# The attention step's turns moved from TensorE to DMA, its order rewritten, and a router of 16 matmuls

## The chip, the cores and the metric

One core of a Trainium2 chip runs the whole kernel. Its engines are TensorE (PE, with its weight loads shown as PEld), VectorE (DVE), ScalarE (ACT), GpSimd (POOL), and SyncE (SP), which here only issues DMAs. The metric is the device time of one execution in microseconds (us), and of several executions the median is given.

## The reference

The input x is 2 x 2048 tokens of 512 channels. It is a block with attention and a mixture of experts side by side, cut here to what matters:

```
xn  = layernorm(x)
# attention: 16 heads of 32, chunks of 128 tokens, decay rate s per head
h   = rmsnorm(xn) * qkv_norm_w ;  qkv = h @ ternary(qkv_w).T
per chunk:  scores = (q k^T) * mask            # decay within a chunk
            o      = scale * (scores v + (q * lam_t) S)
            S      = lam_T * S + (k * lam_rev)^T v
out = rmsnorm(rmsnorm(o) * norm_w) * proj_norm_w @ ternary(proj_w).T
# experts: 8, the best 2 per token; and one shared network of width 1024
probs    = softmax(xn @ w_gate) ; best two, weights renormalised
routed   = sum over the two of  w * ((silu(g) * u) @ w_down),  g, u = xn @ w_gate_up
shared   = (silu(xn @ g_sh) * (xn @ u_sh)) @ w_sh_down
result   = x + out + routed + shared
```

## The kernel before, in words

Matmuls take 16-bit floats for speed; for accuracy each activation is split in a high part and a low rest (both f16). Attention projections multiply both parts with the exact ternary weight. The router and the experts also split their weights and use three of the four products (`PASSES`).

The program has five stages. **Setup** (to about 50 us) makes the ternary weights, the masks and the scaled router weights. **Attention** (50 to about 548 us) runs 16 steps; a step handles chunk n of both batch rows (u = 0, 1), that is 256 tokens, and beside it prepares chunk n+1 (its projections) and n+2 (its layer norm). **Shared, first half** sends eight steps of tokens through the shared network and computes the routing. **Routed** takes 72 tiles of 128 rows, gathered by expert. **Shared, second half** does the other tokens and adds up.

Each engine has an order written out by hand in a function `step(q, par, ...)` (n = 2q + par), and waits are semaphores. An engine never overtakes a waiting instruction of its own list. PE fills three PSUM banks in turn, the ring: the class `Ring` lists the fills of a step in `STEP`, position i takes bank i mod 3, and `fill` makes PE wait until the content three positions earlier has been read. The names are xnT (turned input), kTr (turned keys), ot (outputs), kv (outer products), q, k, v (projections), rt (router), onT (turned normalised output) and proj. Scores have four banks of their own (`sc`), in two pairs; before, a set is four matmuls that fill the first half of a pair's banks, and four sets (`scores(u, ..., sets)`) make one u. `decayed_scores` (VectorE, line 1026) multiplies a set with the mask and writes probs.

Turns. PE turns xn (`xn_turn`, line 624), ScalarE copies xnT, makes hh (line 822) and the high half of x16 (line 814), VectorE makes hl (line 972), GpSimd the low half of x16 (line 1160). The normalised output is turned by `o_turn` (line 727), and `y_high`, `y_low` split it. `masked_kv` (VectorE, line 1043) multiplies the outer products with a block mask. SP's list of a step: load xl of n+2, load xr, store xn, four slices of the expert weights (`load_weights`, whose largest magnitude VectorE takes in `weight_maxima`), store x1 for u = 0, store xT, store x1 for u = 1. In the routed stage GpSimd gathers a tile's 128 rows of xn (f32) by an index copied by VectorE; ScalarE and GpSimd split them in halves (lines 1918, 1850), and SP turns them by DMA (`dma_start_transpose`, line 1823).

## Time and profile before

| what | value |
|---|---|
| median of 3 runs | 1400.04 us (1399.59 to 1403.44) |
| the profiled execution | 1401.92 us, its span 1400.2 us |
| granted clock of TensorE, mean | 0.973 of full speed |
| busy: PE, DVE, ACT, POOL | 91%, 50%, 37%, 38% of the span |
| DMA | 195.06 MB, mean 139 GB/s |

The profile is one execution; a busy time is the time in which an engine worked on an instruction. A group of instructions is named by the line of the kernel that issued it, its engine, and output <- inputs. Matmuls overlap, and the duration shown of one (0.38 us for 512 columns) is longer than the distance from its start to the next one's start; the distance is what it costs.

### The profile page before, as it was taken

The numbers are of one execution on the slowest core, as the hardware profiler recorded it, in microseconds if no ns is written. First come the engines' busy times: TensorE is split into PE (matmuls) and PEld (weight loads), VectorE is DVE, ScalarE is ACT, GpSimd is POOL, SyncE is SP. The second block draws the span as 40 slices with busy tenths as digits, with TensorE's granted clock in tenths as the row PEclk, the third lists the DMA queues.
The fourth block names the chain that finished last, engine by engine and source line by source line (L and its number), as shares of the span: only waits on it lengthen the run. The fifth ranks groups of instructions, "written<-read, shape, count | busy, mean of one in ns | idle before, by whom it ended". The sixth has DMA issues, their size and how long they took to land. (4 is left out here: it accounts for less than half of the span.)

```text
span 1400.2 us, 29499 instructions
## 1 busy us (share of the span) xinstructions
PE 1281.1 (91%) x10418; PEld 879.9 (63%) x10418; DVE 695.2 (50%) x1606; ACT 514.0 (37%) x1034; POOL 527.0 (38%) x467
## 2 busy tenths in 40 slices
PE   1499999999999994999999969999999969999997
PEld 1477777667776673777777734444444447777775
DVE  4477877878878766883333322222222213333323
ACT  3444444444444434432323224544445411111111
POOL 0333344333444332024541035555554542444333
PEclk9699999999999997999999989999999989999999
DMA  5213443334433334524552358888888861443333
GB/s 173 95 60 129 154 145 109 109 131 142 161 109 109 131 125 162 180 93 105 107 138 102 33 136 183 188 194 190 186 191 186 192 190 65 179 164 135 135 136 121
DMA packets 174072, 195.06 MB, mean 139 GB/s; under 512 B 100976, under 2 KB 107248, under 8 KB 174000
## 3 DMA queue, kind: packets, MB, share of 16 engines
q1 hardware_dynamic: 158464, 156.17, 38.0%
q0 software_dynamic: 13328, 37.04, 10.0%
q8 instruction: 55, 0.90, 0.3%
q10 hardware_dynamic: 2208, 0.82, 0.2%
q14 instruction: 17, 0.14, 0.0%
HBM read 117.55 MB, written 56.77 MB: 124 GB/s over the span
## 5 line engine op out<-in xcount | busy, mean ns | idle before, releaser
L1269 PE MATMUL gu<-xT,WG 128*128 128x256 f16 x3072 | 350.3, 275 | 23.5 <-DMA x1s<-x_dram 11.8
L1269 PEld LDWEIGHTS gu<-xT,WG 128*128 128x128 f16 x3072 | 302.7, 99 | 74.8 <-DVE WD L1556 12.4
L1280 PE MATMUL rgu<-WG,raw 128*128 x876 | 215.1, 382 | 14.4 <-issue 10.9
L1695 DVE SCALAR_TENSOR_TENSOR actv<-gu,up_inv,sg 128x512 f32<-128x512 f32 x64 | 48.0, 751 | 252.8 <-ACT sg L1532 252.6
L1532 ACT ACTIVATE sg<-gu,gate_inv 128x512 f32<-128x512 f32 x64 | 43.9, 686 | 319.2 <-PE gu L1269 319.2
L1287 PE MATMUL yp<-WD,ah 128*128 128x512 f16 x512 | 152.3, 379 | 1.0 <-DVE al L1700 1.0
L1280 PEld LDWEIGHTS rgu<-WG,raw 128*128 128x128 f16 x876 | 86.1, 98 | 105.5 <-issue 23.2
L1850 POOL TENSOR_TENSOR xsp<-xg,xsp 128x512 f16<-128x512 f32 x75 | 86.7, 1157 | 105.2 <-ACT xsp L1918 105.2
L655 PE MATMUL ring<-hh,qkvT 128*128 128x256 f16 x512 | 116.4, 276 | 6.0 <-DVE hl L972 6.0
L1250 POOL DMA_INDIRECT xg<-xn_dram,idx x77 | 73.8, 958 | 123.9 <-POOL xsp L1850 66.4
L655 PE MATMUL ring<-hl,qkvT 128*128 128x256 f16 x512 | 116.4, 275 | 0.0
L1765 POOL DMA_INDIRECT raw<-y_dram,gidx x64 | 63.6, 994 | 133.7 <-DVE ys L1676 105.4
L1970 DVE TENSOR_TENSOR alr<-rat,ahr 128x256 f16<-128x256 f32 x72 | 30.5, 424 | 160.0 <-ACT ahr L1938 160.0
L1160 POOL TENSOR_TENSOR x<-xnT,x 128x1024 f16<-128x1024 f32 x16 | 34.3, 2142 | 198.8 <-ACT x L814 198.8
L1749 POOL DMA_INDIRECT slot_dram<-payload,posi x64 | 62.8, 981 | 116.5 <-DVE posi L1645 57.8
L1287 PE MATMUL yp<-WD,al 128*128 128x512 f16 x256 | 97.0, 379 | 0.0
L1026 DVE SCALAR_TENSOR_TENSOR probs<-sc,r,mask 128x512 f32<-128x512 f32 x128 | 89.7, 742 | 3.4 <-PE sc L671 3.4
L1287 PE MATMUL ryp<-WD,ahr 128*128 x288 | 85.9, 379 | 0.0
L1287 PEld LDWEIGHTS yp<-WD,ah 128*128 128x128 f16 x512 | 49.7, 98 | 49.3 <-DVE al L1700 2.5
L1924 ACT ACTIVATE raw<-ryp,out_inv 128x512 f32<-128x512 f32 x72 | 49.5, 687 | 65.9 <-PE ryp L1287 65.9
L1183 POOL TENSOR_TENSOR on<-on,pnw_b 128x512 f32<-128x512 f32 x32 | 40.7, 1273 | 77.1 <-DVE on L1065 77.1
L1700 DVE TENSOR_TENSOR al<-actv,ah 128x512 f16<-128x512 f32 x64 | 46.5, 726 | 44.5 <-ACT ah L1535 44.5
(237 smaller groups left out, 2163.2 us busy)
## 6 DMA issues: line engine op xcount, KB each, us to landing
y_dram<-raw SPq DMA_DIRECT2D x72, 256.0 KB
xl<-in_L_attn_x SPq DMA_DIRECT2D x16, 512.0 KB, 4.5
xn_dram<-xn SPq DMA_DIRECT2D x16, 512.0 KB, 6.4
wraw<-in_L_ffn_w_gate_up SPq DMA_DIRECT2D x16, 512.0 KB, 6.9
xT_dram<-x SPq DMA_DIRECT2D x16, 512.0 KB, 2.8
xr<-in_L_attn_x SPq DMA_DIRECT2D x16, 512.0 KB, 5.9
x_dram<-x SPq DMA_DIRECT2D x32, 256.0 KB, 2.1
xT<-xT_dram SPq DMA_DIRECT2D x16, 512.0 KB, 6.9
```

The lines of the kernel that those rows point to most:

```text
L655: ins = pe.matmul(bank[:, g * T2:(g + 1) * T2], qkvT[:, kk, a:a + P], h[:, kk, :], start=(kk == 0 and h is hh), stop=(kk == KT - 1 and h i ...
L1026: v.scalar_tensor_tensor(out=probs[:, u, s].rearrange("p (j g) t -> p j (g t)", j=2), in0=sc[:, 2 * pair:2 * pair + 2, 0:2 * P], scalar=r[ ...
L1250: pool.indirect_dma_start(out=xg[:, par], out_offset=None, in_=xn_dram, in_offset=bass.IndirectOffsetOnAxis(ap=idx[:, par, 0:1], axis=0)). ...
L1269: ins = pe.matmul(gu[:, h, f * tokens:(f + 1) * tokens], w[:, kk, b, a0:a0 + P], x[:, kk, a], start=(kk == 0 and (a, b) == PASSES[0]), sto ...
L1280: ins = pe.matmul(gu[bank][:], x(kk, a), w[:, 0, kk, b, :], start=(i == 0), stop=(i == len(done) - 1))
L1287: ins = pe.matmul(y[:], act_hl[a][:, f, :], w[:, f, b, :] if len(w.shape) == 4 else w[:, 0, f, b, :], start=(first and f == 0 and (a, b) = ...
L1695: v.scalar_tensor_tensor(out=actv[:, g % 2], in0=gu[g % 2][:, 1].rearrange("p (f t) -> p f t", f=FT), scalar=up_inv[:, 1:2], in1=sg[:], op ...
L1700: v.tensor_tensor(al[:, g % 2], actv[:, g % 2], ah[:, g % 2], ALU.subtract).then_inc(S["al_ready"], 1)
L1749: pool.indirect_dma_start(out=slot_dram, out_offset=bass.IndirectOffsetOnAxis(ap=posi[:, kk, t:t + 1], axis=0), in_=payload[:, kk, t, :], ...
L1765: pool.indirect_dma_start(out=gy[:, u, i], out_offset=None, in_=y_dram, in_offset=bass.IndirectOffsetOnAxis(ap=gidx[:, u, i:i + 1], axis=0 ...
L1850: pool.tensor_tensor(xsp[:, par, 1], xg[:, par], xsp[:, par, 0], ALU.subtract).then_inc(S["low_ready"], 1)
L1924: act.activation(ysb[:, par], yp[par][:], ACT.Copy, scale=out_inv[:, 0:1]).then_inc(S["y_ready"], 1)
```

## The change

All turns in attention are made by DMA. ScalarE, VectorE and GpSimd first write the high and low f16 halves in the untransposed layout side by side (xs for the router and the experts, hs for the projections, ys for proj), and SP issues six DMA transposes of 128 x 1024 f16 in a step: `turn_h` twice, `turn_x` twice, `turn_y` twice. The norm weight of h is now multiplied on GpSimd (`weighted_h`) into hn. The ring loses xnT and onT and gets a new order of 15 names, and the steps of all engines are reordered. A score call is now one pair of whole banks, 8 matmuls, and `decayed_scores` does 1024 elements at once, twice per u. ScalarE copies the diagonal blocks of the outer products (`take_kv`, four copies per u, into kvm cleared once) in place of the masked multiplication on VectorE. The state's decay becomes an operation of its own (`decay`).

The router's matmuls take both halves of its weights side by side as one operand of 16 columns for the high part of x (4 per u) and the high half alone for the low part (4 per u): 16 matmuls for 24. VectorE adds the two sums (`take_logits`), and the scale `ginv` moves into the exponential of the softmax.

The token rows stored for the gather are now the two f16 halves (xs_dram, as many bytes as before). The routed stage gathers them four tiles ahead and turns them directly: the index copies, ScalarE's `high_part` and GpSimd's `low_part` go. In x16, xT_dram and the shared stages the two batch rows u lie apart, so the moving operand of the q, k and shared matmuls is two pieces of 128 columns.

The fragments below come in this order: the ring; SP's new functions and its step; PE's router, scores and step; VectorE's logits, scores and step; GpSimd's weighted_h and step; the routed stage's gather and turn.

```diff
--- before
+++ after
...
     BANKS = 3
-    FRONT = ["xnT0", "xnT1", "q0", "q1", "rt", "k0", "k1", "v0", "v1"]
-    STEP = ["xnT0", "xnT1", "kTr0", "ot0", "kv0", "q0", "q1", "kTr1", "ot1", "rt", "onT0", "k0", "kv1", "k1", "proj0",
-            "onT1", "v0", "v1", None, None, "proj1"]
-    LAST = ["kTr0", "ot0", "kv0", "kTr1", "ot1", "onT0", "kv1", "proj0", "onT1", "proj1"]
+    FRONT = ["q0", "q1", "rt", "k0", "k1", "v0", "v1", None, None]
+    STEP = ["kTr0", "ot0", "kTr1", "kv0", "ot1", "q0", "q1", "k0", "rt", "k1", "v0", "proj0", "kv1", "v1", "proj1"]
+    LAST = ["kTr0", "ot0", "kTr1", "kv0", "ot1", "proj0", "kv1", "proj1"]
...
+            def turn_h(q, par):
+                n = 2 * q + par
+                if not (isinstance(n, int) and n == 0):
+                    wait_apart(sp, S["v_ready"], 2 * n, S["sp_passed"])
+                for u in range(B):
+                    wait_apart(sp, S["hl_ready"], 2 * n + u + 1, S["sp_passed"])
+                    sp.dma_start_transpose(hT[:, u], hs[:, u].rearrange("p a c -> p (a c)")).then_inc(hT_in[u], 16)
+            def turn_x(q, par):
+                n = 2 * q + par
+                if not (isinstance(n, int) and n < 2):
+                    wait_apart(sp, S["logits_ready"], n - 1, S["sp_passed"])
+                    wait_apart(sp, xT_out[par], 16 * q, S["sp_passed"])
+                for u in range(B):
+                    wait_apart(sp, S["xlow_ready"], 2 * n + u + 1, S["sp_passed"])
+                    sp.dma_start_transpose(x16[:, par, u], xs[:, u].rearrange("p a c -> p (a c)")).then_inc(xT_in[u], 16)
...
+            def turn_y(u, q, par):
+                n = 2 * q + par
+                wait_apart(sp, S["yl_ready"], 2 * n + u + 1, S["sp_passed"])
+                sp.dma_start_transpose(yT[:, u], ys[:, u].rearrange("p a c -> p (a c)")).then_inc(yT_in[u], 16)
...
                 if norm:
                     sp.wait_ge(S["xn_ready"], 2 * n + 2)
                     load_xl(q + 1, par)
-                if not front:
+                if front:
+                    turn_h(*after(q, par))
+                    turn_x(*after(q, par))
+                    store_xs(*after(q, par))
+                    sp.wait_ge(S["wmax_ready"], n)
+                    load_weights(*after(q, par))
+                else:
                     for g in range(2):
                         load_group(sp, k, g)
                 sp.wait_ge(S["x1_ready"], 2 * n)
                 load_xr(q, par)
+                for u in range(B):
+                    turn_y(u, q, par)
+                store_x1(0, q, par)
                 if front:
-                    store_xn(*after(q, par))
-                    sp.wait_ge(S["wmax_ready"], n)
-                    load_weights(*after(q, par))
-                for u in range(B):
-                    if u == 1 and front:
-                        store_xT(*after(q, par))
-                    sp.wait_ge(S["x1_ready"], 2 * n + u + 1)
-                    dst = x1_steps[n] if isinstance(n, int) else x1_steps[bass.ds(n, 1)][0]
-                    sp.dma_start(dst[:, u], x1[:, u]).then_inc(x1_out[u], 16)
+                    store_xT(*after(q, par))
+                store_x1(1, q, par)
...
             def router(q, par, st):
                 n = 2 * q + par
-                pe.wait_ge(S["xlow_ready"], n + 1)
+                for u in range(B):
+                    pe.wait_ge(xT_in[u], 16 * (n + 1))
                 bank, done = fill(pe, "rt", st)
                 for u in range(B):
+                    both = slice(2 * u * EXPERTS, 2 * (u + 1) * EXPERTS)
                     for kk in range(KT):
-                        for i, (a, b) in enumerate(PASSES):
-                            ins = pe.matmul(bank[:, u * EXPERTS:(u + 1) * EXPERTS], x16[:, par, kk, a, u * P:(u + 1) * P],
-                                            wg16[:, kk, b, :], start=(kk == 0 and i == 0), stop=(kk == KT - 1 and i == 2))
+                        pe.matmul(bank[:, both], x16[:, par, u, kk, :], wg16[:, kk].rearrange("p b e -> p (b e)"),
+                                  start=(kk == 0), stop=False, skip_group_check=True)
+                    for kk in range(KT):
+                        ins = pe.matmul(bank[:, 2 * u * EXPERTS:(2 * u + 1) * EXPERTS], x16[:, par, u, KT + kk, :],
+                                        wg16[:, kk, 0, :], start=False, stop=(kk == KT - 1), skip_group_check=True)
                 ins.then_inc(done, 1)
...
-            def scores(u, q, par, sets):
-                n = 2 * q + par
-                if u == 0 and sets[0] == 0:
+            def scores(u, q, par, pair):
+                n = 2 * q + par
+                if u == 0 and pair == 0:
                     pe.wait_ge(S["q_ready"], 2 * n + 2)
                     pe.wait_ge(S["k_ready"], 2 * n + 2)
-                for s in sets:
-                    pair = s % 2
-                    pe.wait_ge(sc_free[pair], 4 * n + 2 * u + s // 2)
-                    for gg in range(2):
-                        for jj in range(2):
-                            g, j = 2 * (s // 2) + gg, 2 * pair + jj
-                            rows = slice(HD * j, HD * j + HD)
-                            ins = pe.matmul(sc[:, j, gg * P:(gg + 1) * P], kT[rows, par, g, u * P:(u + 1) * P],
-                                            qT[rows, par, g, u * P:(u + 1) * P], start=True, stop=True)
-                    ins.then_inc(sc_full[pair], 1)
+                pe.wait_ge(sc_free[pair], 2 * n + u)
+                for g in range(KT):
+                    for j in (2 * pair, 2 * pair + 1):
+                        rows = slice(HD * j, HD * j + HD)
+                        ins = pe.matmul(sc[:, j, g * P:(g + 1) * P], kT[rows, par, g, u * P:(u + 1) * P],
+                                        qT[rows, par, g, u * P:(u + 1) * P], start=True, stop=True)
+                ins.then_inc(sc_full[pair], 1)
...
                 nxt = after(q, par)
-                if front:
-                    xn_turn(0, *nxt, st)
-                    xn_turn(1, *nxt, st)
                 k_turn(0, q, par, st)
-                scores(1, q, par, (0, 1))
+                scores(1, q, par, 0)
                 outputs(0, q, par, st)
-                scores(1, q, par, (2, 3))
+                scores(1, q, par, 1)
+                k_turn(1, q, par, st)
+                o_back(0, q, par)
                 outer(0, q, par, st)
-                o_back(0, q, par)
+                outputs(1, q, par, st)
                 if front:
                     project("q0", *nxt, st)
+                o_back(1, q, par)
+                if front:
                     project("q1", *nxt, st)
-                k_turn(1, q, par, st)
-                outputs(1, q, par, st)
+                    project("k0", *nxt, st)
+                    router(*nxt, st)
+                    project("k1", *nxt, st)
+                    project("v0", *nxt, st)
+                    scores(0, *nxt, 0)
+                proj(0, q, par, st)
                 if front:
-                    router(*nxt, st)
-                o_back(1, q, par)
-                o_turn(0, q, par, st)
-                if front:
-                    project("k0", *nxt, st)
+                    scores(0, *nxt, 1)
                 outer(1, q, par, st)
                 if front:
-                    project("k1", *nxt, st)
-                proj(0, q, par, st)
-                if front:
-                    scores(0, *nxt, (0, 1))
-                o_turn(1, q, par, st)
-                if front:
-                    project("v0", *nxt, st)
-                    scores(0, *nxt, (2, 3))
                     project("v1", *nxt, st)
                 proj(1, q, par, st)
...
                 bank = filled(v, "rt", st)
                 dst = logits[:, :, n, :] if isinstance(n, int) else logits[:, :, bass.ds(n, 1), :][:, :, 0, :]
-                v.tensor_scalar(dst, bank[:, 0:B * EXPERTS].rearrange("p (u e) -> p u e", u=B), ginv[:, 0:1], None, ALU.mult
-                                ).then_inc(S["logits_ready"], 1)
+                parts = bank[:, 0:2 * B * EXPERTS].rearrange("p (u b e) -> p u e b", u=B, b=2)
+                v.tensor_reduce(dst, parts, AX.X, ALU.add).then_inc(S["logits_ready"], 1)
...
-                    v.wait_ge(sc_full[pair], 4 * n + 2 * u + s // 2 + 1)
-                    v.scalar_tensor_tensor(out=probs[:, u, s].rearrange("p (j g) t -> p j (g t)", j=2),
-                                           in0=sc[:, 2 * pair:2 * pair + 2, 0:2 * P],
+                for pair in range(2):
+                    v.wait_ge(sc_full[pair], 2 * n + u + 1)
+                    v.scalar_tensor_tensor(out=probs[:, u, pair].rearrange("p j g t -> p j (g t)"),
+                                           in0=sc[:, 2 * pair:2 * pair + 2],
                                            scalar=r[:, par, u:u + 1],
-                                           in1=mask[:, 4 * s:4 * s + 4].rearrange("p (j g) t -> p j (g t)", j=2),
+                                           in1=mask[:, 8 * pair:8 * pair + 8].rearrange("p (j g) t -> p j (g t)", j=2),
                                            op0=ALU.mult, op1=ALU.mult).then_inc(sc_free[pair], 1)
...
                 scaled_k(0, q, par, st)
-                decayed_scores(1, q, par, (0, 1))
-                if front:
-                    h_low(*nxt)
-                decayed_scores(1, q, par, (2, 3))
-                weight_maxima(q, par, (1, 2, 3))
-                masked_kv(0, q, par, st)
+                decayed_scores(1, q, par)
                 o_mean(0, q, par)
+                scaled_k(1, q, par, st)
                 normed(0, q, par)
                 if has_norm:
                     row_stats(0, q + 1, par)
                     row_stats(1, q + 1, par)
-                scaled_k(1, q, par, st)
-                second_norm(0, q, par)
+                weight_maxima(q, par, (1, 2, 3))
+                o_mean(1, q, par)
+                if has_norm:
+                    norm_stats(q + 1, par)
+                normed(1, q, par)
+                y_low(0, q, par)
+                weight_maxima(q, par, (0,))
+                for u in range(B):
+                    second_norm(u, q, par)
+                for u in range(B):
+                    second_factor(u, q, par)
                 if front:
                     take_logits(*nxt, st)
-                y_low(0, q, par, st)
-                o_mean(1, q, par)
-                normed(1, q, par)
+                y_low(1, q, par)
                 if has_norm:
-                    norm_stats(q + 1, par)
-                masked_kv(1, q, par, st)
-                second_norm(1, q, par)
-                weight_maxima(q, par, (0,))
+                    norm_factors(q + 1, par)
+                    norm(q + 1, par)
+                residual(0, q, par, st)
                 if front:
-                    decayed_scores(0, *nxt, (0, 1))
-                residual(0, q, par, st)
-                if has_norm:
-                    norm(q + 1, par)
-                y_low(1, q, par, st)
-                if front:
-                    decayed_scores(0, *nxt, (2, 3))
+                    decayed_scores(0, *nxt)
                 else:
                     weight_scales()
+                if has_norm:
+                    h_low(q + 1, par)
                 residual(1, q, par, st)
-                if has_norm:
-                    norm_factors(q + 1, par)
...
+            def weighted_h(q, par):
+                n = 2 * q + par
+                for u in range(B):
+                    pool.wait_ge(S["xn_ready"], 2 * n + u + 1)
+                    if not (isinstance(n, int) and n == 0):
+                        pool.wait_ge(S["hl_ready"], 2 * n + u - 1)
+                    pool.tensor_tensor(hn[:, u], xn[:, par, u], hw_b[:], ALU.mult).then_inc(S["hn_ready"], 1)
...
                     x_low(*after(q, par))
+                decay(0, q, par)
                 weighted(0, q, par)
+                decay(1, q, par)
+                weighted(1, q, par)
                 update(0, q, par)
+                if norm:
+                    weighted_h(q + 1, par)
                 if front:
                     decayed_q(*after(q, par))
-                weighted(1, q, par)
                 update(1, q, par)
...
+        def gather(pool, r):
+            pool.indirect_dma_start(out=xg[:, r % XG], out_offset=None, in_=xs_dram,
+                                    in_offset=bass.IndirectOffsetOnAxis(ap=slots[:, r, 0:1], axis=0)
+                                    ).then_inc(xg_in[r % XG], 16)
...
                                     in_=payload[:, kk, t, :], in_offset=None).then_inc(slot_out, 16)
-                        for par in range(2):
-                            gather(pool, 0, par, S["pool_passed"])
+                        pool.wait_ge(split, PIECES * (GROUPS + EXPERTS - 1))
+                        pool.wait_ge(slot_in, 16)
+                        for r in range(XG):
+                            gather(pool, r)
...
-                        wait_apart(sp, S["low_ready"], r + 1, S["sp_passed"])
-                        sp.dma_start_transpose(xh[:, i % XH], xsp[:, i % 2].rearrange("p a c -> p (a c)")
-                                               ).then_inc(turned[i % 2], 16)
...
```

## Rows read from the trace of the kernel before

**Rows 1.** The page: busy us of each engine, share, instructions.
```profile
PE 1281.1 (91%) x10418; PEld 879.9 (63%) x10418; DVE 695.2 (50%) x1606; ACT 514.0 (37%) x1034; POOL 527.0 (38%) x467
```

**Rows 2.** Windows: length, busy us (instructions) of each engine, clock, DMA share, GB/s.
```profile
822.00:1112.00 290.00, 286.36 (x1374) 137.66 (x1375) 74.56 (x274) 140.47 (x273) 144.92 (x137) 0.99 0.83 185
...
79.48:519.93 440.45, 423.84 (x4674) 320.12 (x4674) 347.88 (x836) 197.62 (x463) 173.45 (x120) 1.00 0.36 125
```

**Rows 3.** Order of time, PE, one attention step: start, us, then the instruction.
```profile
343.32 1.04 PE L624 MATMUL ring<-ident,xn 128*128 128x128 f32 x8
344.33 0.66 PE L679 MATMUL ring<-ident,kT 128*128 128x128 f32 x4
344.91 0.74 PE L671 MATMUL sc<-qT,kT 32*128 32x128 f32 x16
345.58 1.16 PE L689 MATMUL ring<-qlam,state 128*128 128x128 f32 x8
...
349.79 0.27 PE L655 MATMUL ring<-hh,qkvT 128*128 128x256 f16 x1
...
353.28 0.60 PE L679 MATMUL ring<-ident,kT 128*128 128x128 f32 x4
...
355.71 0.76 PE L634 MATMUL ring<-wg,x 128*128 128x8 f16 x24
356.50 0.66 PE L709 MATMUL o_ps<-ident,oT 128*128 128x128 f32 x4
356.99 0.60 PE L727 MATMUL ring<-ident,on 128*128 128x128 f32 x4
357.43 0.27 PE L655 MATMUL ring<-hh,qkvT 128*128 128x256 f16 x1
...
364.31 0.66 PE L727 MATMUL ring<-ident,on 128*128 128x128 f32 x4
364.80 0.38 PE L648 MATMUL ring<-qkvT,hh 128*128 128x512 f16 x1
...
366.88 1.37 PE L671 MATMUL sc<-qT,kT 32*128 32x128 f32 x16 [0.19 <-DVE probs L1026]
...
368.29 0.38 PE L648 MATMUL ring<-qkvT,hh 128*128 128x512 f16 x1
...
369.79 0.38 PE L648 MATMUL ring<-qkvT,hl 128*128 128x512 f16 x1
...
371.04 0.38 PE L736 MATMUL ring<-projT,yh 128*128 128x512 f16 x1 [0.87 <-ACT vS L832]
```

**Rows 4.** Groups by line: xcount | busy us, mean ns, then idle before.
```profile
L1026 DVE SCALAR_TENSOR_TENSOR probs<-sc,r,mask 128x512 f32<-128x512 f32 x128 | 89.7, 742 | 3.4 <-PE sc L671 3.4
...
L1183 POOL TENSOR_TENSOR on<-on,pnw_b 128x512 f32<-128x512 f32 x32 | 40.7, 1273 | 77.1 <-DVE on L1065 77.1
...
L988 DVE TENSOR_REDUCE wmax<-wraw 128x1024 f32 x12 | 14.5, 1206 | 0.0
```

**Rows 5.** DMA: transposes on SP; queue in 900 to 950, then 330 to 390.
```profile
L1823 SPq DMA_TRANSPOSE raw<-xsp x75: 1232/1246/2240, 816.6 to 1128.0; - x75
...
DMA to landing us min/median/max: 3.0/3.1/5.2
...
q1 hardware_dynamic: 14358, 6.28, 58.8%
...
q1 hardware_dynamic: 3648, 7.60, 36.9%
```

**Rows 6.** Start of the routed stage, PE and SP; PE's waits in it.
```profile
822.16 6.48 PE L1280 MATMUL rgu<-WG,raw 128*128 x18 [10.89 <-issue]
...
816.58 15.87 SPq L1823 DMA_TRANSPOSE raw<-xsp  x4
...
PE rgu L1280 <- DMA raw<-xsp: 3.4, 7, 0.8
```

**Rows 7.** Order of time, PE, first projection of the attention block.
```profile
61.49 0.39 PE L655 MATMUL ring<-hh,qkvT 128*128 128x256 f16 x1 [5.99 <-DVE hl L972]
```

414 lines of the change are left out of this document (184 added, 230 removed).

## Prediction

> **What bounds the kernel now.** I read the page's busy times first [rows 1]: TensorE (PE) works 91% of the span, no other engine more than half. An average hides stages, so next the windows by stage [rows 2]: from the first attention step's k_turn to the last one's, PE is busy 423.84 of 440.45 us at the full 2.4 GHz (granted clock 1.00), and in the routed stage 286.36 of 290.00 (0.99). Both stages are PE's. DMA's share is 0.36 in the first and 0.83 in the second. Hence a removed PE instruction is worth its issue time, and work put on other engines is free until it makes PE wait. Third, the order of time inside one attention step [rows 3]. The window of rows 2 holds 15 steps, so one takes 29.36 us. It shows what PE does, start to start, and the only two stalls: before the fourth score set and before proj1. I say once: about 0.3% (4 us) is what a measurement here can tell from none.
>
> **Part 1, PE work of one step, all from [rows 3].** xn_turn goes: 343.32 to 344.33, 1.01 us. The two o_turns go: 356.99 to 357.43 and 364.31 to 364.80, 0.93 us. The router: 24 matmuls from 355.71 to 356.50 are 0.033 us each; 16 leave 0.53, so 0.26 us less. The bound from below is the same 0.79 (no gain, if 16 columns cost double); it is a quarter microsecond either way. Scores: a free set of 8 matmuls takes 344.91 to 345.58, 0.67 us; the one in front of v1 takes 366.88 to 368.29, 1.41, waiting in its middle for VectorE's probs. The new pairs use whole banks with two row groups alternating, as inside a set now, so I take 0.67: 0.74 less. v0 starts at 364.80, is 8 matmuls at 0.215 (368.29 to 369.79 is seven), and so ends 366.52; scores start at 366.88. Of this gap 0.2 goes. proj1 waits for ScalarE to empty v1's bank: v1 ends at 370.01, proj1 starts at 371.04, 1.03 us. In the new ring proj1 is index 14 and takes the bank of proj0 (11), which residual(0) read long before. It goes whole. The sum is 4.17 us. From 29.4 that leaves PE 25.3 us.
>
> **Part 2, the other engines in those 25.3 us.** VectorE's h_low becomes two full-width operations, at most 0.74 each like a probs operation [rows 4]; masked_kv leaves it; eight probs operations of 742 ns become four of twice the width (bounds 0.74 and 1.48; a weight maximum over 1024 elements takes 1206 ns [rows 4], and I take 1.28 as the nearest). It was busy about 23 us a step and comes to about 21. GpSimd gains weighted_h, 2 of on's shape at 1273 ns, 2.5 us on some 11.7: 14.2. ScalarE takes take_kv (eight small copies, at most 0.4 each) for the two xnT and some scaled copies: even. None is a bound. I also followed the lists by hand: VectorE makes ys(0) ready about 15 us into a step, ScalarE has every bank empty when PE asks (k1 and v0 with under 1 us to spare), GpSimd's qlam is ready about 1 us before outputs(0). These are estimates with little slack.
>
> **Part 3, the DMA turns; here lies the uncertainty.** A step gains six transposes of 256 KB on SP's queue. In the routed stage, in 50 us, the hardware queue was busy 58.8% (29.4 us) with 12 transposes and 13 stores [rows 5]. Plain transfers move 7.60 MB in 36.9% of 60 us, 343 GB/s, so a 256 KB store is 0.76 us, 13 are 9.9, and a transpose is (29.4-9.9)/12 = 1.63 us of all 16 engines. Issue to landing is 3.1 us, 1.25 of it SP's [rows 5]. So the six cost 9.8 us beside plain traffic of 11.1 (22.1 over two steps): 20.9 us in 25.3, a share of 0.83. The routed stage carries just that share and PE loses little [rows 2, 6]. SP itself issues six at 1.25 and ten plain at about 0.5: 12 us, room enough.
> The row and a rule differ here. The Trainium skill (Advanced Engine Details and Errata, X-Bar Transpose (TRN2)) says transposes are as fast as regular DMAs; by that each is 0.76 us, the queue never makes PE wait, and the result would be rival B's. The trace disagrees, with 1.63 beside 0.76, but in a stage where gathers share the engines.
> What matters is order. SP's list is strict, and one queue serves in turn. SP enters step n only when residual(1) of n-1 is done, about 1.2 us after PE started n (VectorE still has h_low for u = 1 ahead of it, which waits for ScalarE to take v1). I put the first bytes at about 2.7, an estimate: the issue and half of what lies between a transpose's issue end and its landing. Service by then: x1 0.76, xl 1.5, two hT, two xT, xs 1.5, the four weight slices (1.18 MB) 3.4, xr 1.5, then yT(0). PE asks for hT (q0) at 7.9: today k_turn(0) to q0 is 344.33 to 349.79, 5.46, and k_turn(1) with outputs(1), which now stand ahead of q0 too, is 353.28 to 355.71, 2.43 [rows 3]. hT lands at 2.7+2.26+2x1.63 = 8.2: 0.3 late. PE asks for yT(0) at 18.4 (q0 with q1 is 349.79 to 353.28, 3.49; k0 with k1 the same; o_back 0.5, router 0.53, v0 1.72, scores 0.67). It lands at 2.7+8.66+5x1.63 = 19.5: 1.1 late, the first included. yT(1) has 4 us slack. So the step becomes 25.3+1.1 = 26.4 in strict order and 25.3 if the order is softer; I take 26.2. In general it is 25.3 + max(0, 5s-7.0) for a transpose of s us.
> Gain: 15 x (29.36-26.2) = 47.4 us.
>
> **Part 4, the ends.** Start: today q0 begins 61.49, after a wait of 5.99 for hl [rows 7]. New: xn 53.0, hn by GpSimd 1.27 twice, hs high and low, two transposes with nothing ahead of them (wraw is behind turn_x): about 60.4. Step 0 then has its weight loads late. I put 0, bounds -1.5 to +3. Last step: yT(0) sits behind 3 MB of group weights, and proj(0) then runs cold; but residual(1) waits for the weight scales chain anyway. +1, bounds 0 to +4. Routed start: PE begins at 822.16 after 10.89 idle; the first transpose is issued at 816.58 [rows 6], behind ACT's and GpSimd's split of the gathered rows; now it can go as soon as SP has issued the block's two loads: -1.1, bounds -0.3 to -2.5. Routed steady state: GpSimd's and ScalarE's splitting of each tile's rows leaves; neither sets PE's pace, only the 3.4 us that PE waited for a transpose, 7 times [rows 6]: -1, bounds +1 (transposes unchanged) to -3.4. Everything else I cost at nothing: ginv moves into the exponential's scale, bmask and qnw_c are setup work behind weight loads, ten index copies are gone from VectorE. The two-piece moving operand (2 x 128) in the q, k and 3072 shared matmuls I also put at 0: each piece is still unit stride. Its upper bound, taken as slow as one of xn_turn's 128-column transposes (8 in 1.01, 0.126 each) instead of the 0.109 of q's 32 in 3.49 [rows 3], is +52 us for the shared part.
>
> **Sum.** 47.4 - 0 - 1 + 1.1 + 1 = 48.5 us less. Against the profiled execution's own 1401.92 (span 1400.2): 1353.4. The median of the runs is 1400.04, 1.9 below it: 1351.5, say 1352.
>
> **Rivals.** A, the forecast: transposes just late, step 25.8 to 26.9; 1342 to 1362; 0.46.
> B: transposes cost nearly what plain transfers cost or overlap them, step 25.3 (5s-7.0 negative): 15 x 4.06 = 60.9 gained, 1338. For it: the 3.1 us landing is flat even at share 0.83. 0.22.
> C: the queue or a chain with little slack (qlam, k1's bank) costs 2 to 3.5 us a step, step 27.3 to 28.8: 1368 to 1391, centre 1378. For it: landing reached 5.2 us at most [rows 5], and bursts cluster at each step's start. 0.20.
> D, slower than before: the transposes throttle the queue. Every step's hT and yT hang on SP's strict list, which waits for the last residual, so lateness is paid in each step and not made up. It passes today's 29.36 once 5s-7.0 exceeds 4.1, s = 2.2 us. At s = 2.6 the step is 31.3 and the time 1429. Against it: the measured 1.63 includes contention. 0.08.
> E: the two-piece operand costs half its bound in the shared stages, +25: 1377. Nothing in the trace speaks for it. 0.04.
> Likeliest is A: 1352. The range 1336 to 1378 takes B, A and the better half of C. Slower by over 0.3%: most of D, 0.07; within: 0.03; faster: 0.90.
>
> **What the changed profile would show.** Step period (k_turn to k_turn) about 26.2, PE idle in it 1 us, released by the DMAs of hT and yT and not by ACT vS; no stall at proj1; scores 0.67 both times; router 0.53. DMA share in attention 0.75 to 0.85. Routed tiles at the same pace, PE starting about 1 us sooner after its gap. Shared matmuls still spaced 0.109. I am wrong if PE waits there for probs, kS or the state, or if hT lands after 9 us into the step.

## The result, and the profile after

The median is 1360.03 us (4 runs, 1358.43 to 1364.50) against 1400.37 us for the kernel before in the same session (4 runs, 1399.59 to 1403.44). The ratio is 0.9713, with a 95% interval of 0.9686 to 0.9741: faster, by 40 us. The forecast was 1352, with a range of 1336 to 1378 and 0.90 on faster. The profiled execution took 1360.6 us, its span 1358.8, at a mean granted clock of 0.975.

The page's busy times, to be read beside [rows 1]:

```profile
PE 1252.2 (92%) x10034; PEld 865.4 (64%) x10034; DVE 648.2 (48%) x1396; ACT 479.2 (35%) x1039; POOL 488.3 (36%) x437
```

Windows of the same two stages as [rows 2], each from its first to its last matmul or k_turn:

```profile
790.47:1095.80 305.33, 302.75 (x1452) 146.26 (x1452) 74.12 (x216) 110.59 (x215) 64.33 (x68) 0.99 0.79 181
...
78.03:482.91 404.88, 401.61 (x4321) 309.27 (x4321) 306.57 (x716) 201.28 (x538) 218.76 (x163) 1.00 0.74 197
```

The 15 steps take 404.88 us, 26.99 each, where they took 440.45, 29.36 each. PE is busy in all but 3.3 us of them, so the step is almost pure PE work, and DMA's share has doubled to 0.74. PE's waits from 80 to 490 us are these two alone:

```profile
PE ring L751 <- DMA yT<-ys: 2.8, 4, 1.2
PE ring L682 <- issue: 0.5, 1, 0.5
```

Order of time on PE, beside [rows 3]; the first four lines are of the step whose k_turn is at 322.21, the others of the next one, whose k_turn is at 348.95:

```profile
322.21 0.60 PE L704 MATMUL ring<-ident,kT 128*128 128x128 f32 x4
322.74 1.16 PE L696 MATMUL sc<-qT,kT 32*128 32x128 f32 x16
323.83 1.16 PE L714 MATMUL ring<-qlam,state 128*128 128x128 f32 x8
...
330.84 1.37 PE L682 MATMUL ring<-hT,qkvT 128*128 128x256 f16 x11
...
363.27 0.25 PE L657 MATMUL ring<-wg,x 128*128 128x16 f16 x4
363.38 0.24 PE L660 MATMUL ring<-wg,x 128*128 128x8 f16 x4
...
363.68 1.91 PE L682 MATMUL ring<-hT,qkvT 128*128 128x256 f16 x16
...
368.33 1.90 PE L751 MATMUL ring<-projT,yT 128*128 128x512 f16 x8
```

Three things stand here. A score set takes 322.74 to 323.83, 1.09 us, where a free set took 0.67 [rows 3]. The router takes 363.27 to 363.68, 0.41 (forecast 0.53). And q0 starts 8.63 us into the step. SP's queue in the same step tells how near the edge that is:

```profile
323.49 0.33 SPq L589 DMA_DIRECT2D x_dram<-x  x1
324.03 0.41 SPq L552 DMA_DIRECT2D xl<-in_L_attn_x  x1
324.76 2.96 SPq L567 DMA_TRANSPOSE hT<-hs  x2
...
337.03 4.22 SPq L606 DMA_TRANSPOSE yT<-ys  x2
```

The second transpose of hs is issued at 326.2, and the longest of the two landings is 4.2 us: hT is there at 330.4, 0.4 us ahead of q0. That is 8.2 us into the step, as forecast. In the 9 us around yT the 16 DMA engines are taken nearly all the time (window 334 to 343, DMA share 0.97; the share is a sum of packet times and reads up to 1.25 in a stretch of another run below, so 1 is not a hard ceiling):

```profile
334.00:343.00 9.00, 9.00 (x88) 6.56 (x87) 7.33 (x30) 4.99 (x15) 4.18 (x3) 1.00 0.97 238
```

The span's 41.4 us are divided so, read from PE's first instructions of each stage:

| stage | change, us | forecast |
|---|---|---|
| up to the first k_turn (79.48, now 78.03) | -1.5 | 0 |
| 15 steps | -35.6 | -47.4 |
| last step, k_turn to the first shared matmul (35.65, now 40.35) | +4.7 | +1 |
| shared stages, both halves | -0.7 | 0 |
| gap ahead of the routed stage (10.89, now 11.68) | +0.8 | -1.1 |
| routed tiles | -0.7 | -1 |
| gap behind the routed stage (11.71, now 3.24) | -8.5 | 0 |

The last step, on PE:

```profile
499.90 3.31 PE L751 MATMUL ring<-projT,yT 128*128 128x512 f16 x8 [6.92 <-DMA yT<-ys]
503.05 1.05 PE L742 MATMUL ring<-vS,kS 128*128 128x128 f32 x8
503.94 1.89 PE L751 MATMUL ring<-projT,yT 128*128 128x512 f16 x8
523.26 1.01 PE L1294 MATMUL gu<-xT,WG 128*128 128x256 f16 x4 [17.43 <-DMA x1s<-x_dram]
```

GpSimd and VectorE in the same stretch:

```profile
505.39 1.26 POOL L1203 TENSOR_TENSOR state<-state,kvm 128x512 f32<-128x512 f32 x1 [6.44 <-ACT kvm L855]
512.89 0.39 POOL L1233 PARTITION_ALL_REDUCE wall<-wtop  x1 [6.24 <-issue]
```

```profile
503.92 0.21 DVE L1022 TENSOR_REDUCE wtop<-wmax 128x4 f32<-128x64 f32 x1
513.32 0.17 DVE L1024 TENSOR_SCALAR wall<-wall 128x4 f32<-128x4 f32 x1 [9.19 <-POOL wall L1233]
```

VectorE has the maxima ready at 504.1, but GpSimd still has its last state update, which hangs on outer(1), behind the late proj(0). The all-reduce shows 6.24 us after that update, and residual(1), the store and the reload of x1 stand behind it. In the kernel before, the update was done at 539.4, ahead of wtop, and VectorE waited 5.06 us:

```profile
538.11 1.27 POOL L1178 TENSOR_TENSOR state<-state,kvm 128x512 f32<-128x512 f32 x1
545.20 0.39 POOL L1201 PARTITION_ALL_REDUCE wall<-wtop  x1 [5.82 <-issue]
```

```profile
540.36 0.20 DVE L1004 TENSOR_REDUCE wtop<-wmax 128x4 f32<-128x64 f32 x1
```

The gap behind the routed stage, PE, after:

```profile
1099.20 2.08 PE L1294 MATMUL gu<-xT,WG 128*128 128x256 f16 x13 [3.24 <-PEq L1803]
```

### The profile page after: what moved, and what is told of

Its sections match the earlier page's. It is cut to its first block and busy times, and to the rows that moved or that the text cites. A ratio compares the mean times of both kernels' runs of the same rounds, so it can differ in the third digit from the quotient of the medians.

```text
span 1358.8 us, 27803 instructions
## 1 busy us (share of the span) xinstructions
PE 1252.2 (92%) x10034; PEld 865.4 (64%) x10034; DVE 648.2 (48%) x1396; ACT 479.2 (35%) x1039; POOL 488.3 (36%) x437
## 5 line engine op out<-in xcount | busy, mean ns | idle before, releaser
L1275 POOL DMA_INDIRECT raw<-xs_dram,slots x73 | 69.2, 948 | 295.9 <-DMA raw<-raw 238.6
L682 PE MATMUL ring<-hT,qkvT 128*128 128x256 f16 x1024 | 121.6, 275 | 19.7 <-DMA hT<-hs 19.3
L682 PEld LDWEIGHTS ring<-hT,qkvT 128*128 128x128 f16 x1024 | 98.6, 99 | 34.8 <-issue 22.9
L1043 DVE SCALAR_TENSOR_TENSOR probs<-sc,r,mask 128x1024 f32<-128x1024 f32 x64 | 80.5, 1279 | 35.7 <-PE sc L696 35.3
L1208 POOL TENSOR_TENSOR on<-on,pnw_b 128x512 f32<-128x512 f32 x32 | 46.8, 1463 | 101.4 <-DVE on L1075 101.4
L696 PE MATMUL sc<-qT,kT 32*128 32x128 f32 x1024 | 73.6, 283 | 0.7 <-issue 0.7
L696 PEld LDWEIGHTS sc<-qT,kT 32*128 32x128 f32 x1024 | 61.7, 186 | 19.5 <-issue 19.5
L1946 DVE SCALAR_TENSOR_TENSOR actvr<-rgu,cw,sgr 128x256 f32<-128x256 f32 x72 | 34.8, 484 | 78.5 <-ACT sgr L1921 78.5
```

The lines of the kernel that those rows point to most:

```text
L682: ins = pe.matmul(bank[:, g * T2:(g + 1) * T2].rearrange("p (u t) -> p u t", u=B), qkvT[:, kk, w0:w0 + P], hT[:, :, a * KT + kk, :], start ...
L696: ins = pe.matmul(sc[:, j, g * P:(g + 1) * P], kT[rows, par, g, u * P:(u + 1) * P], qT[rows, par, g, u * P:(u + 1) * P], start=True, stop= ...
L1043: v.scalar_tensor_tensor(out=probs[:, u, pair].rearrange("p j g t -> p j (g t)"), in0=sc[:, 2 * pair:2 * pair + 2], scalar=r[:, par, u:u + 1],
L1208: pool.tensor_tensor(on3[:, u], on[:, u], pnw_b[:], ALU.mult).then_inc(S["on3_ready"], 1)
L1275: pool.indirect_dma_start(out=xg[:, r % XG], out_offset=None, in_=xs_dram, in_offset=bass.IndirectOffsetOnAxis(ap=slots[:, r, 0:1], axis=0 ...
```

## The experiments

All ratios are to the kernel before. In the listings by step, the period is the first k_turn to the sixteenth, over 15.

**Score sets.** A set in the kernel after runs 8 matmuls of 32 rows over two row groups (j) of the array; the sets before used all four in one call. Two kernels change the order alone. In the first, both pairs go as one run of 16 matmuls:

```diff
                 for g in range(KT):
-                    for j in (2 * pair, 2 * pair + 1):
+                    for j in range(HPT):
...
-                ins.then_inc(sc_full[pair], 1)
+                        if g == KT - 1 and j % 2 == 1:
+                            ins.then_inc(sc_full[j // 2], 1)
```

> The changed kernel with the two score pairs of one u issued as one run of 16 matmuls, g outside and all four row groups j = 0..3 inside; VectorE's operations stay. Theory R (the score sets grew from 0.67 to 1.09 us because a call now alternates between two row groups only, where it went over all four before): the 16 matmuls take about 1.1 us in place of 2 x 1.09, the step falls from 26.75 to 24.6 if no other wait appears, 1325 us in all; VectorE and the turn of y are then within 0.5 us of the path, so up to 1335. Rival W (the price comes from filling whole banks, or from 128 columns of 32 rows as such): 16 matmuls still take 2.2 us, step 26.7, 1360 us.

Measured: 1357.98 us, ratio 0.9689 (0.9664 to 0.9714). Its order of time on PE:

```profile
321.70 1.17 PE L697 MATMUL sc<-qT,kT 32*128 32x128 f32 x32
322.80 1.16 PE L716 MATMUL ring<-qlam,state 128*128 128x128 f32 x8
...
330.75 1.91 PE L682 MATMUL ring<-hT,qkvT 128*128 128x256 f16 x16 [1.61 <-issue]
```

Sixteen matmuls take 1.10 us, as long as eight did. So the mechanism holds, and 2.2 us of PE work a step are gone. But the time hardly moves (2 us, less than the intervals of the two kernels), and the period is 27.09 (76.56 to 482.98): the saved time is now a wait of q0, 24.8 us in 13 waits from 80 to 480 us. The view names no releaser for it (`issue`), but the weight load beside it waits for the DMA of hT. The second kernel lets neighbours share a row group:

```diff
-                for g in range(KT):
-                    for j in (2 * pair, 2 * pair + 1):
+                for j in (2 * pair, 2 * pair + 1):
+                    for g in range(KT):
```

> The changed kernel with the two loops of a score call exchanged: j outside, g inside, so that neighbours in the queue use the same row group. Theory R: two row groups overlapped before, now hardly any; a call takes 1.6 to 1.75 us in place of 1.09, step 26.75 + 4 x 0.6 = 29.1, about 1397 us. Rival W (nothing overlapped in the changed kernel anyway): unchanged, 1.09 us and 1360 us.

Measured, in a single run: 1390.72 us, period 28.94 (78.75 to 512.90), no PE wait. A set:

```profile
368.74 1.71 PE L696 MATMUL sc<-qT,kT 32*128 32x128 f32 x16
```

So 8 such matmuls cost 1.7, 1.09 or 0.55 us with one, two or four row groups in turn. The Trainium skill (TensorE: Matmul & The Clock Gate, Why this matters for your kernels) says small-K matmuls run concurrently when each lands in a distinct row group, with a factor of 3.07 for four; the trace agrees, with 1.71 over 0.55.

**The last step.** outer(1) and ScalarE's copies of kv(1) go ahead of proj(0) and of y_high(1), in the last step only:

```diff
-    LAST = ["kTr0", "ot0", "kTr1", "kv0", "ot1", "proj0", "kv1", "proj1"]
+    LAST = ["kTr0", "ot0", "kTr1", "kv0", "ot1", "kv1", "proj0", "proj1"]
...
+                if not front:
+                    outer(1, q, par, st)
                 proj(0, q, par, st)
...
+                if not front:
+                    take_kv(1, q, par, st)
                 y_high(1, q, par)
```

> The changed kernel with, in the last attention step only, outer(1) ahead of proj(0) on TensorE (kv1 before proj0 in the ring) and take_kv(1) ahead of y_high(1) on ScalarE. Theory L: the last step lost 4.7 us because GpSimd's all-reduce of the weight maxima comes 6.2 us after its last state update, which waited for outer(1), which waited behind proj(0) for the turned y. Then the all-reduce starts 4 to 6 us sooner and the time is 1355. Rival Y (the turned y itself ends the stage): proj(1) and residual(1) stay the end and the time stays 1360.

Measured: 1349.94 us, ratio 0.9640 (0.9622 to 0.9657). GpSimd's last update and all-reduce:

```profile
502.25 1.26 POOL L1207 TENSOR_TENSOR state<-state,kvm 128x512 f32<-128x512 f32 x1 [0.32 <-ACT kvm L857]
509.30 0.39 POOL L1237 PARTITION_ALL_REDUCE wall<-wtop  x1 [5.78 <-issue]
```

From k_turn to the first shared matmul it is now 33.6 us (485.89 to 519.49) in place of 40.35, although proj(0) starts no earlier. The order was the cause of the 4.7, and 2 us more were there to be had. The medians say 10 us, this stretch 6.7; the rest isn't placed. The profiled execution is the slowest of that kernel's five (1356.53 us), and its last k_turn came 3 us later than in the kernel after.

**SP's list.** What held hT in the first experiment? The row of SP there has hT issued at 325.60, 4.43 us after k_turn, behind the store of x1(1) (324.33) and the load of xl (324.86); in the kernel after it was 2.55. The store waits for residual(1), which ends VectorE's list behind probs and h_low. VectorE at the end of that step (the next k_turn is at 347.58):

```profile
343.60 0.75 DVE L1104 SCALAR_TENSOR_TENSOR x<-ring,g,xr 128x512 f32<-128x512 f32 x1 [1.71 <-PE ring L753]
344.27 2.47 DVE L1041 SCALAR_TENSOR_TENSOR probs<-sc,r,mask 128x1024 f32<-128x1024 f32 x2
346.65 3.26 DVE L990 TENSOR_TENSOR hs<-raw,hs 128x512 f16<-128x512 f32 x2
349.84 0.74 DVE L1104 SCALAR_TENSOR_TENSOR x<-ring,g,xr 128x512 f32<-128x512 f32 x1
```

VectorE waits for proj(0) on PE and then works through to residual(1) without a gap; v1 and ScalarE's part of hs don't hold it. Its two h_low operations take 3.26 us here and 1.92 in the kernel after: GpSimd works beside them nearly all the time here and under half of it there.

First both edits together, without touching SP:

> The kernel after with both earlier edits: score pairs as 16 matmuls over four row groups, and in the last step outer(1) and its copies ahead of proj(0) and y_high(1). Theory A (the two edits act in different places and add): the steps keep the period of the four-group kernel, 26.41 us with q0 waiting for hT, and the shared stage starts about 10 us earlier; 1360 - 2 - 10 = 1348 us. Theory B (the shorter last step of the second edit gave its gain only because that kernel's other steps ran late): 1355 us or more.

Measured: 1348.79 us, ratio 0.9647 (0.9629 to 0.9664), period 27.01. The score order is again worth 1 us, which is less than the intervals can tell, and the two edits together are worth what the shorter last step is worth alone. (The 26.41 in the expectation was one step, read off a timeline; the mean over 15 of that kernel is 27.09.) Now SP turns hs for the step after next as soon as it is there:

```diff
                 if front:
-                    turn_h(*after(q, par))
+                    if isinstance(q, int) and n == 0:
+                        turn_h(0, 1)
                     turn_x(*after(q, par))
...
                 if front:
                     store_xT(*after(q, par))
+                if norm:
+                    turn_h(q + 1, par)
                 store_x1(1, q, par)
```

> As the kernel with both edits, and SyncE issues the two transposes of hs for the step after next ahead of the store of x1(1) and of the load of xl, not behind them. In the four-group kernel x1(1) was ready at 323.43, its store went out at 324.33 and hT was issued at 325.60, while hs was whole about 322.8. Theory S (SyncE's list in strict order behind residual(1) makes hT late): hT is issued about 2 us earlier, the wait of q0 (1.6 to 2.5 us at 13 of 15 steps) is gone or under 0.5, the period falls from 26.41 to 25.1 to 25.8, and the time is 9 to 18 us below the kernel with both edits: 1330 to 1339. Theory T (the time that the transposes take under load, or VectorE and ScalarE that make hs, set hT): q0 still waits over 1 us, period over 26.1, 1344 to 1350.

Measured: 1324.99 us, ratio 0.9461 (0.9446 to 0.9477). SP in one step, whose k_turn is at 329.57:

```profile
329.63 2.93 SPq L567 DMA_TRANSPOSE hT<-hs  x2
332.85 0.34 SPq L589 DMA_DIRECT2D x_dram<-x  x1
333.89 0.40 SPq L552 DMA_DIRECT2D xl<-in_L_attn_x  x1
```

And the window of its 15 steps:

```profile
77.32:455.01 377.69, 370.83 (x4321) 281.16 (x4321) 314.45 (x716) 202.11 (x538) 228.54 (x163) 1.00 0.81 211
```

hT is issued 0.06 us into this step and within 1.3 us of k_turn in the others, q0 no longer waits, and the period is 25.18. The list was the wait. What PE still waits for in the 15 steps is mostly yT, 4.3 us in 7 waits. One could still think that ScalarE's order of making hs is next, so the high half of h(0) was put ahead of the copies of kv(1):

> As the last one, and ScalarE takes the high half of h(0) ahead of the copies of kv(1) (1.10 us). If VectorE and ScalarE that make hs are what holds hT after SyncE's order is mended, another 0.2 to 1 us per step goes, 3 to 15 us in all. If not, it is the same within 3 us, or up to 5 us slower, because kvm(1) and with it GpSimd's update of the state come 0.6 us later.

Measured: 1324.36 us, ratio 0.9460 (0.9437 to 0.9484), period 25.14: the same. And the fourth corner, SP's new order with the old score sets:

> The shorter last step and SyncE's transposes of hs ahead of the store of x1(1), but the score sets as in the kernel after (8 matmuls over two row groups each). It is the fourth corner of a square: scores in sets or pairs, SyncE's order old or new. Known corners, all with the shorter last step: sets and old order 1350, pairs and old order 1349, pairs and new order 1325. Theory S (in the kernel after PE's own 26.99 us per step hide a late hT; only when the scores are shorter does SyncE's order show): 1350 within 2 us, period 26.9 to 27.0, so neither edit is worth anything alone and both together 24 us. Rival (the order alone pays, because it also calms the transfers around yT or the other queues): 1335 to 1345.

Measured: 1351.45 us, ratio 0.9654 (0.9627 to 0.9680), period 26.78. With the shorter last step in all four, the square is:

| | SP's order of after | hs turned first |
|---|---|---|
| score sets, two row groups | 1349.94 | 1351.45 |
| score pairs, four row groups | 1348.79 | 1324.99 |

Neither edit alone is worth anything that the intervals can tell, both together 25 us. Two bounds of 27 us lay on top of each other: PE's own work, and the loop q0, proj(0), residual(0), probs and h_low, residual(1), SP's list, hT, q0. That the order of SP's list is the weak link of the loop is shown by the square; its other links are read from the rows above.

**What a transpose costs.** Two more per step, of a constant tile into a spare one, in the kernel after:

```diff
                     turn_x(*after(q, par))
+                    turn_spare(0, n)
                     store_xs(*after(q, par))
...
                 load_xr(q, par)
+                if front:
+                    turn_spare(1, n)
                 for u in range(B):
                     turn_y(u, q, par)
```

> The kernel after with two more transposes of the same shape per step (of a constant tile into a spare one that nobody reads), one behind those of x, one ahead of those of ys: eight in place of six. The prediction put one at 1.63 us of all 16 engines: 3.3 us per step more on 19.97 (0.74 of 26.99), so the DMA share rises from 0.74 to 0.84 to 0.86, yT lands 1.3 us or more later against a slack of some 1.1 us, proj(0) waits 0.3 to 1.5 us in most steps, and the time rises by 5 to 22 us to 1365 to 1382. Rival (transposes are cheap, half of that or less): share 0.77 to 0.80, no wait, 1360 within 3 us.

Measured: 1424.97 us, ratio 1.0174 (1.0158 to 1.0191): slower than the kernel before, and far above the 1365 to 1382 expected. Its windows over the 15 steps, over the wait for one late proj(0) and over that proj(0), then PE's order of time there:

```profile
77.00:548.30 471.30, 433.31 (x4321) 321.12 (x4322) 306.61 (x716) 201.16 (x538) 218.01 (x163) 0.92 0.74 186
...
352.60:354.70 2.10, 0.00 (x0) 0.00 (x1) 0.31 (x1) 0.00 (x0) 2.09 (x2) 1.00 1.25 261
354.70:358.30 3.60, 3.60 (x10) 1.13 (x11) 0.00 (x0) 0.00 (x0) 2.85 (x2) 0.53 0.12 23
```

```profile
349.60 1.89 PE L687 MATMUL ring<-qkvT,hT 128*128 128x512 f16 x8
...
354.70 3.56 PE L763 MATMUL ring<-projT,yT 128*128 128x512 f16 x8 [2.12 <-DMA yT<-ys]
```

The period is 31.42: 4.4 us more, of which the wait in front of proj(0) is 2.1 here, and 1.7 is that the eight matmuls behind it take 3.49 (354.70 to 358.19) and not 1.8. The granted clock of that stretch is 0.53, so the engine is at 1.2 of its two levels (1.2 and 2.4 GHz) for nearly all of it. By the windows of all 15 steps, PE idles 2.3 us a step more than in the kernel after and is busy 2.1 us more with the same matmuls. One part of the lateness isn't load: the second spare transpose stands ahead of ys in SP's own list too, and yT is issued at 348.91, 15.8 us after k_turn in place of 14.8. With one more transpose only, behind those of x:

> The kernel after with one more transpose per step, behind those of x; none directly ahead of those of ys. With two more (the second directly ahead of ys) each step was 4.4 us longer and the time 65 us. Theory O (what stands directly ahead of ys in the queue decides: its 16 engines are 0.97 busy from 334 to 343 us of the kernel after, and less before that): the extra work drains ahead of ys, proj(0) waits 0 to 0.3 us, and the time is 1360 to 1366. Theory L (the load of all transfers decides, each transpose alike): half of the 65 us or near it, proj(0) waits in most steps, 1385 to 1395. In both the DMA busy time per step rises by 1.6 to 1.8 us.

Measured: 1384.89 us, ratio 0.9888 (0.9869 to 0.9906). PE waits 17.6 us for yT in 14 waits from 80 to 480 us, and the window of its steps is:

```profile
77.95:506.30 428.35, 408.98 (x4321) 311.68 (x4322) 306.51 (x716) 201.16 (x538) 218.28 (x163) 0.98 0.76 195
```

DMA busy time per step is share times period. With the share of the queue to three digits over the same windows it is 0.740 x 26.99 = 19.97 us in the kernel after, 0.755 x 28.56 = 21.56 with one more and 0.735 x 31.42 = 23.09 with two. One transpose is 1.6 us of all 16 engines; the forecast had 1.63. That it costs twice a plain transfer isn't only contention: in the trace of the kernel after, over the 15 steps, a transpose is 1024 packets of 256 bytes at a mean of 22.9 ns, 1.47 us over 16 engines, and the plain packets of 2048 bytes beside them take 96 ns each, 0.77 us for 256 KB. The load is what decides, not what stands directly ahead of yT: SP issues yT 14.8 us after k_turn (353.32 behind 338.50) as in the kernel after, it takes 4.9 us in the median to land where it took 3.6, and still PE waits. There is no room for a seventh. The step grows by 1.57 us with the first and by 2.86 more with the second, where yT's later issue and more slow matmuls behind the wait come on top.

**The router.** 24 matmuls again, nothing else changed:

```diff
-                        pe.matmul(bank[:, both], x16[:, par, u, kk, :], wg16[:, kk].rearrange("p b e -> p (b e)"),
-                                  start=(kk == 0), stop=False, skip_group_check=True)
+                        for b in range(2):
+                            pe.matmul(bank[:, (2 * u + b) * EXPERTS:(2 * u + b + 1) * EXPERTS], x16[:, par, u, kk, :],
+                                      wg16[:, kk, b, :], start=(kk == 0 and b == 0), stop=False, skip_group_check=True)
```

> The kernel after with the router as 24 matmuls of 16 columns instead of 16 of 32 and 16. Theory R (PE's work sets the period, and the router's matmul count is what costs): the router takes 0.79 us as in the kernel before instead of 0.40, 16 times 0.39 = 6 us more: 1366 us. Rival (the router's time hides in something else, or PE is not what sets the period): 1360 within 2 us.

Measured: 1363.71 us, ratio 0.9736 (0.9723 to 0.9749). The router takes 0.61 us there, 0.20 more, where 0.39 was expected; 16 x 0.20 = 3.3 us would answer to the 3.7 measured, but the intervals of the two kernels overlap, so the price rests on the rows. Each of the matmuls takes 0.025 us there as in the kernel after, where it took 0.033 in the kernel before. So of the router's own gain of 0.38, from 0.79 to 0.41, 0.20 is the lower count and 0.18 comes with the new order of operands and results; which of these does it is not shown.

**The bank of proj1, in the kernel before.** Only its place in the ring changes:

```diff
-            "onT1", "v0", "v1", None, None, "proj1"]
+            "onT1", "v0", "v1", None, "proj1", None]
```

> The kernel before with proj1 one place earlier in the ring of banks, so that its bank is the one of v0 and not the one of v1. Theory P (the 1.03 us that PE waits ahead of proj(1) in each step is only the bank's): the stall goes, a smaller wait of some 0.4 us for the bank of the next step takes its place, so 0.5 to 0.9 us per step, 8 to 14 us in all: 1386 to 1392. Rival (something else ends last in that place): 1400 within 3 us.

Measured: 1394.06 us, ratio 0.9949 (0.9934 to 0.9965), period 28.80. PE's waits from 80 to 480 us:

```profile
PE ring L624 <- DVE x L1093: 6.5, 13, 0.5
PE sc L671 <- DVE probs L1026: 2.3, 12, 0.2
```

Of the 1.03 us, 0.56 are gained, and most of the rest turns into a wait for VectorE to empty the bank that the next step's xnT takes, 6.5 us in 13 waits. The wait for probs is as in the kernel before. The gain is 6.6 us, a little short of the 8 to 14 expected.

**The gap behind the routed stage.** GpSimd's last row gather of the kernel before started at 1128.78, when PE had ended the stage; the tiles gathered ahead are never used. The kernel after has its last one at 1071.73. One surplus gather is put back at the end:

```diff
+                    pool.wait_ge(S["al_ready"], SLOT_TILES)
+                    gather(pool, TURNS)
+                    pool.wait_ge(xg_in[TURNS % XG], 16 * (TURNS // XG + 1))
```

> The changed kernel with one more gather of rows on GpSimd that starts when the last routed tile's al is ready, and is waited for at the end of the stage, as the kernel before does with its surplus gathers. Its rows are not used. Theory G: the gap between the routed stage and the second shared stage, 12.1 us before and 3.6 now, was that late gather; it comes back to about 12, +8 us, 1368. Rival X (the surplus transposes, ScalarE's surplus high parts or the loops that are no longer there made the gap): gap 4 to 6 us, 1360 to 1362.

Measured: 1368.92 us, ratio 0.9769 (0.9744 to 0.9795), 9 us above the kernel after.

```profile
1107.07 5.14 PE L1294 MATMUL gu<-xT,WG 128*128 128x256 f16 x30 [8.63 <-PEq L1803]
```

PE's gap is 8.63 in place of 3.24. So a late gather explains 5.4 of the 8.5 us. The kernel before waited 11.71 there. Of the 3.1 between the two, 1.9 is that the gather put back starts 1.4 us ahead of the end of PE's routed work (1097.00 and 1098.44), and the one of the kernel before started 0.5 us behind it (1128.78 and 1128.30); the last 1.2 stay open. Of the 9 us in the medians, the profiled execution has some 2.6 inside the routed stage (308.1 us in place of 305.5), for which no cause is shown.

## Why the prediction was right, and where it was not

The sign, the stage and the range were right. 1360 is inside rival A's 1342 to 1362, but by luck: A's step was 25.8 to 26.9 and the measured one is 26.99, PE's own work and not the late transposes of A fills it, and 8.5 us behind the routed stage that nobody forecast made up for it. Step by step:

- **PE's work per step, 4.17 removed, 25.3 left: the term that was mis-sized is the scores.** The prediction took 0.67 us for a set, since it had "two row groups alternating, as inside a set now". The call before that it timed held two sets on four row groups; one set on two measures 1.09. Four times 0.42 is +1.68 per step. The router came out at 0.41 for 0.53, -0.12. 29.36 - 4.17 is 25.19, which the prediction wrote as 25.3; 25.19 + 1.68 - 0.12 = 26.75, against 401.61 / 15 = 26.77 of busy time measured, and 0.2 of waits. The other terms stand together, and the stall at proj1 is gone; that it "goes whole" was true here, and was 0.56 of 1.03 where nothing else changed.
- **The transposes, 1.63 us each: right.** The two kernels with more of them give 1.6. Rival B, cheap transposes, is out, as each costs twice the 0.76 us of a plain transfer. By this the rule of the Trainium skill (Advanced Engine Details and Errata, X-Bar Transpose (TRN2)) that the prediction weighed doesn't hold in this kernel. hT landed at 8.2 as forecast; yT(0), issued at 14.8 and landing at 19.2 at the latest, was forecast at 19.5.
- **The stall of about 1 us a step: not paid.** The longer score sets moved PE's asking for hT from 7.9 to 8.6 and for yT from 18.4 to 19.4, past both landings in most steps; 4 waits for yT, 2.8 us in all, remain. The two errors partly cancel: 26.2 forecast, 26.99 measured.
- **A step the prediction didn't have.** It fixed SP's entry at 1.2 us after k_turn for any PE. That is so at 27 us a step; with PE's work cut to 24.8 (four row groups) hT is issued 4.4 us after k_turn and the period stays at 27. Had the sets cost 0.67 as forecast, this loop would still have held the step at about 26.7 and not 26.2. That is an estimate: the 27.09 less the 0.42 of the one set between q0 and proj(0), in which the loops of the two kernels are alike (10.7 us). It is in the prediction only as rival D's mechanism ("SP's strict list, which waits for the last residual, so lateness is paid in each step"), and its floor was not worked out.
- **Rival D's threshold** was right in kind: the change lies at an edge. It was reached not by s = 2.2 but by 8 transposes of 1.6, and about half through the clock.
- **Rival C, 2 to 3.5 us a step from the queue or a chain: did not come.** PE waits 0.2 us a step. The other engines' busy times were right: 20.4, 14.6 and 13.4 us a step on VectorE, GpSimd and ScalarE.
- **Last step, +1 (bounds 0 to +4): +4.7.** "residual(1) waits for the weight scales chain anyway" was right, but the chain itself was delayed, through GpSimd's state update behind outer(1).
- **Routed start, -1.1:** it did not come (+0.8), and the trace shows where it went. The first transpose is issued 1.1 us sooner as forecast (783.04, 4.2 us behind PE's last matmul, where it was 816.58 and 5.3), but it takes 5.8 us to land and not 4.3: it now goes out 0.5 us behind the block's second load, where 1.6 us lay between them.
- **Two-piece operand, 0: right.** Both shared stages keep their length within 0.7 us in all. Rival E is out.
- **Behind the routed stage, nothing forecast, -8.5 came.** Without it the time would have been 1368, at the near end of rival C. The miss of the total is 7 us in the profiled execution: +11.8 (steps), +3.7 (last step), +1.9 and +0.3 (routed), less 8.5, 1.5 (start) and 0.7 (shared).

## What to carry to other kernels

When a step is bound by one engine, work out the closed loops through the other lists and the DMA queue too, with their period: the loop, and not the engine's sum, can be the next floor, and two bounds of equal length hide each other's edits until both are made. In a strict DMA list, put the transfer that the next step asks for first ahead of stores that wait for this step's last result. And take the price of a small matmul from rows with the same row groups in the same order, for one and the same instruction cost 0.07, 0.14 or 0.21 us.

The last point bears on where to go from here: the kernel with the three edits (four row groups, hs turned first, shorter last step) beats both, 1325.0 us against 1360.0 and 1400.4.

## What the runs showed of the hardware that was not expected

- More DMA load can be paid in full though the queue isn't full: one transpose more per step, 1.6 us of engine time, made the step 1.57 us longer, at a mean DMA share of only 0.74 to 0.76. The mean hides the 9 us at 0.97.
- A PE wait of 2.1 us was followed by matmuls at nearly half speed (3.49 us for 1.8) in the kernel with two more transposes, with the granted clock at 0.53 meanwhile. With one more, that happened behind the waits of 1.36, 1.50, 1.98 and 2.28 us (proj(0) took 2.8 to 3.5), and not behind the other eleven, of 0.2 to 1.9 us (1.83). So the length of the wait alone doesn't tell.
- VectorE's h_low operation (128x512, f32 to f16) takes 0.69 us when GpSimd is all but idle beside it and 1.64 when GpSimd works all the while (kernel after and the one with four row groups).
- The partition all-reduce of GpSimd starts 5.7 to 6.2 us after the operation ahead of it in the traces of all 14 kernels, while its input had been ready for 1.1 us (both edits), 1.8 (shorter last step), 4.6 (before) or 8.8 (after). So it is what stands ahead of it on GpSimd that sets its start.
